# A transformer block in fp4 emulation on one core: negated scales made by GpSimd, ten zero products, the last tile normalised by VectorE, every queue re-sorted

## What is computed

```python
def reference(out, W_write, W_read, decay, log_alpha, w_gate, w_up, w_down):
    x = out                                     # (8, 512, 256) float32
    # chunked linear attention with a decay, read by r = x, written by w = x shifted by one
    v = x @ W_write.T
    reads = decayed_causal(x, shifted(x)) @ v   # scan over chunks in the reference
    attn = x + exp(log_alpha) * (reads @ W_read.T)
    x = layernorm(x + attn)
    # feed-forward, each operand rounded to fp4 blockwise (16 values share a scale)
    gate, y = fp4(x) @ fp4(w_gate).T, fp4(x) @ fp4(w_up).T     # 704 columns each
    h = silu(gate) * y
    return layernorm(x + fp4(h) @ fp4(w_down).T)
```

## Time and profile before

| | |
|---|---|
| median of 3 runs | 326.65 us (326.39 to 327.18) |
| the profiled execution, own time | 326.19 us |
| span of that execution in the profile | 324.5 us |
| instructions in the profile | 6515 |
| TensorE busy | 314.7 us, 97% |
| VectorE busy | 293.5 us, 90% |
| GpSimd busy | 239.9 us, 74% |
| ScalarE busy | 210.8 us, 65% |
| read from and written to HBM | 11.08 MB and 4.19 MB |

### The profile page before, as it was taken

One profiled execution on the slowest core, in us unless ns is written; L12 is line 12 of the kernel. 1 busy time (PEld: TensorE's weight loads), 2 busy tenths in 40 slices (PEclk: granted clock), 3 DMA queues, 4 the chain that ended last, 5 costly groups with the idle time before them and its releaser, 6 DMA issues.

```text
span 324.5 us, 6515 instructions
## 1 busy us (share of the span) xinstructions
PE 314.7 (97%) x2065; PEld 285.2 (88%) x2065; DVE 293.5 (90%) x754; ACT 210.8 (65%) x516; POOL 239.9 (74%) x257
## 2 busy tenths in 40 slices
PE   8999999999999999999999999999999999999993
PEld 3899888979988999899999999899989889999983
DVE  4999898999898999698996989999999999999982
ACT  7378977594915786348926687466657745665774
POOL 1869859857975789956996688687677767569672
PEclk9999999999999999999999999999999999999999
DMA  6821300210010202020010200020000000001002
GB/s 230 295 67 67 128 3 0 68 66 2 1 65 18 82 2 75 24 81 20 32 68 16 83 1 33 2 81 17 18 2 33 18 0 33 19 16 34 33 31 69
DMA packets 8242, 15.69 MB, mean 48 GB/s; under 512 B 1040, under 2 KB 5136, under 8 KB 8208
## 3 DMA queue, kind: packets, MB, share of 16 engines
q1 hardware_dynamic: 7920, 15.01, 13.5%
q10 hardware_dynamic: 288, 0.26, 0.3%
HBM read 11.08 MB, written 4.19 MB: 47 GB/s over the span
## 4 chain that ended last, share of the span: by engine, by line
PE 70%; DVE 18%; issue 6%; ACT 4%; POOL 1%; DVEq 0%; POOLq 0%; ACTq 0%
PE gu L1690 11%; PE gu L1694 11%; PE gu L1691 11%; PE bank L1690 5%; PE bank L1691 5%; PE bank L1694 5%; PE bank L1778 4%; DVE h_y L1071 3%; PE bank L1700 2%; PE bank L1703 2%; PE bank L1704 2%; DVE w_raw L1182 2%; PE bank L1752 2%; PE gu L1825 2%; DVE hqT_lo L1209 2%
## 5 line engine op out<-in xcount | busy, mean ns | idle before, releaser
L410 POOL TENSOR_TENSOR h_q<-h_g,h_ns 128x704 f32<-128x704 f32 x32 | 47.3, 1477 | 39.5 <-DVE h_g L1076 36.0
L1690 PE MATMUL gu<-guT_hi,xqT_hi 128*128 128x512 f32 (+1 forms) x192 | 74.9, 390 | 0.5 <-DVE w_raw L1182 0.5
L1691 PE MATMUL gu<-guT_lo,xqT_hi 128*128 128x512 f32 (+1 forms) x192 | 72.1, 376 | 0.0
L681 ACT ACTIVATE w_raw<-gu 128x512 f32<-128x512 f32 x64 | 29.3, 461 | 47.2 <-PE gu L1694 46.8
L1694 PE MATMUL gu<-guT_hi,xqT_lo 128*128 128x512 f32 (+1 forms) x192 | 56.7, 377 | 0.5 <-DVE xqT_lo L1173 0.5
L403 POOL TENSOR_TENSOR h_n<-w_raw,h_rs 128x704 f32<-128x704 f32 x32 | 49.0, 1531 | 9.3 <-DVE h_rs L1066 8.8
L1690 PEld LDWEIGHTS gu<-guT_hi,xqT_hi 128*128 128x128 f32 x192 | 36.1, 188 | 6.7 <-issue 1.3
L1694 PEld LDWEIGHTS gu<-guT_hi,xqT_lo 128*128 128x128 f32 x192 | 35.6, 188 | 6.7 <-DVE xqT_lo L1173 0.9
L1691 PEld LDWEIGHTS gu<-guT_lo,xqT_hi 128*128 128x128 f32 x192 | 36.2, 188 | 5.2
L1071 DVE SCALAR_TENSOR_TENSOR h_y<-h_sq,h_n 128x704 f32<-128x704 bf16 x34 | 36.3, 1069 | 1.6 <-ACT h_sq L685 1.5
L1182 DVE TENSOR_TENSOR w_raw<-w_raw,gu 128x512 f32<-128x512 f32 x64 | 32.3, 506 | 2.9 <-ACT w_raw L681 2.2
(11 more groups left out here) (156 smaller groups left out, 941.1 us busy)
## 6 DMA issues: line engine op xcount, KB each, us to landing
xs<-in_x_rows_dram SPq DMA_DIRECT2D x8, 512.0 KB, 3.3
out_dram<-wq_gu SPq DMA_DIRECT2D x32, 128.0 KB, 1.7
x_full<-in_xt_rows_dram SPq DMA_DIRECT2D x7, 512.0 KB, 3.3
w_raw<-in_w_ffn_dram SPq DMA_DIRECT2D x6, 352.0 KB, 5.9
w_pair<-in_w_attn_dram SPq DMA_DIRECT2D x1, 512.0 KB, 5.1
x_full<-in_xt_rows_dram SPq DMA_DIRECT2D x1, 256.0 KB, 2.8
x_full<-in_xt_rows_dram ACTq DMA_DIRECT2D x1, 256.0 KB, 3.4
scal<-in_scalars_dram ACTq DMA_DIRECT2D x1, 1.0 KB, 1.7
```

The lines of the kernel that those rows point to most:

```text
L410: nc.gpsimd.tensor_tensor(blocks(h_q[:, p, 0:I]), blocks(h_g[:, p, :]), per_block(h_ns[:, p, :], HB), ALU.mult).then_inc(h_quant, 1)
L681: nc.scalar.activation(silu[:, p, part[half]], gate_of[half], ACT.Silu).then_inc(silu_ready, 1)
L1690: nc.tensor.matmul(dst, lh, rh, start=(first and i == 0), stop=False)
L1691: nc.tensor.matmul(dst, lh, rl, start=False, stop=False)
```

## The change

1. `h_ns` is made by GpSimd in a new step `h_neg_scales`; `h_divisors` on VectorE makes `h_sc` alone. The wait for the dequantisation of two tiles before moves from `h_divisors` to `h_neg_scales`, `h_maxima` waits for the negation of two tiles before as well, and `h_dequant` waits for the negation of its own tile.
2. Ten products of zeros in place of 14.
3. The last tile (31) is normalised by VectorE in a new step `out_finish`, which adds the negated mean and multiplies by the power's result; GpSimd makes only the power for this tile, and the last store waits for `out_finish`.
4. The bank tables are changed (`combine` goes to `bank[0]`), and the lists on all engines, SP's loads included, are re-sorted. The steps themselves and their number stay, apart from the above.

```diff
-        s_bank, r_bank = (gu[:, 3, :], bank[0], bank[3], gu[:, 3, :]), (bank[2], bank[1])
-        h_bank = ((bank[1], bank[0]), (bank[1], bank[0]), (bank[2], gu[:, 3, :]), (bank[3], gu[:, 3, :]))
-        d_bank = (bank[3], bank[0], bank[2], gu[:, 3, :])
+        s_bank, r_bank = (bank[3], gu[:, 3, :], bank[0], gu[:, 3, :]), (bank[0], bank[3])
+        h_bank = ((bank[3], gu[:, 3, :]), (bank[1], bank[2]), (bank[0], gu[:, 3, :]), (bank[0], bank[2]))
+        d_bank = (bank[3], bank[2], bank[1], bank[0])
...
-            store(31, 3)
+            sp.wait_ge(o_last, 1)
+            sp.dma_start(out_rows[31], o_out[:, 3, :]).then_inc(stored[3], 16)
...
+            def h_neg_scales(k, p):
+
+                pool.wait_ge(h_amax, k + 1)
+                if k >= 2:
+                    pool.wait_ge(h_quant, k - 1)
+                nc.gpsimd.tensor_scalar(h_ns[:, p, :].rearrange("p (r c) -> p r c", c=4), h_am[:, p, :, 0:4], -1.0 / FP4_MAX,
+                                        -SCALE_FLOOR, ALU.mult, ALU.min).then_inc(h_negated, 1)
+
             def h_dequant(k, p):
                 pool.wait_ge(h_grid, k + 1)
+                pool.wait_ge(h_negated, k + 1)
...
-            out_rstd(31, 1)
+            pool.wait_ge(o_var, 32)
+            nc.gpsimd.tensor_tensor(o_rstd[:, 1:2], o_ve[:, 1:2], neg_half[:, 0:1], ALU.pow).then_inc(o_rstd_ready, 1)
...
                 if k >= 2:
                     dve.wait_ge(h_div, k - 1)
+                    dve.wait_ge(h_negated, k - 1)
...
             def h_divisors(k, p):
-                if k >= 2:
-                    dve.wait_ge(h_quant, k - 1)
-                divisors(h_am[:, p, :, 0:4], h_sc[:, p, :], h_ns[:, p, :], h_amax, h_div, k + 1)
+                dve.wait_ge(h_amax, k + 1)
+                nc.vector.tensor_scalar(rows_like(h_sc[:, p, :], h_am[:, p, :, 0:4]), h_am[:, p, :, 0:4], NUDGE / FP4_MAX,
+                                        SCALE_FLOOR * NUDGE, ALU.mult, ALU.max).then_inc(h_div, 1)
...
+            def out_finish(k, b, t):
+
+                p = t % 2
+                c = slice(p, p + 1)
+                dve.wait_ge(o_var, k + 1)
+                dve.wait_ge(o_rstd_ready, k + 1)
+                dve.wait_ge(stored[t], b * 16 + 16)
+                nc.vector.tensor_scalar(o_out[:, t, :], o_z[:, p, :], o_nm[:, c], o_rstd[:, c], ALU.add,
+                                        ALU.mult).then_inc(o_last, 1)
...
-            for _ in range(14):
+            for _ in range(10):
                 nc.tensor.matmul(gu[:, 3, :], zeros[:, 0:P], zeros[:], start=True, stop=True)
...
             gate_up(31, 7, 3, 0)
+            h_transpose(27, 3, 1, [(o_ready, 26)])
+            down(26, 2, [(hT_lo_ready, 51)])
             gate_up(31, 7, 3, 1)
```

More of the change, by code:

```diff
@@ L1384, in _ @@
-            out_moments(0, 0)
-            h_rest(2, 2, 0)
-            x_divisors(2, 1)
-            h_rest(2, 2, 1)
+            hidden(4, 0, 0)
+            h_magic_add(2, 0)
+            x_to_grid(1, 1)
+            hidden(4, 0, 1)
+            out_residual(0, 0)
+            h_rest(1, 1, 0)
+            h_reciprocals(3, 1)
+            h_to_grid(2, 0)
+            h_maxima(4, 0)
+            hidden(5, 1, 0)
+            x_residual(3, 0)
+            x_divisors(2, 0)
+            h_divisors(4, 0)
@@ new lines, in _ @@
+            x_to_grid(6, 1)
+            hidden(23, 1, 0)
+            hidden(23, 1, 1)
+            x_residual(7, 1)
+            h_to_grid(21, 1)
+            h_magic_add(22, 0)
+            out_residual(18, 2)
+            h_rest(19, 3, 0)
+            h_maxima(23, 1)
+            h_rest(19, 3, 1)
+            h_divisors(23, 1)
+            x_reciprocals(7, 0)
+            h_reciprocals(23, 1)
+            h_rest(20, 0, 0)
+            out_residual(19, 3)
+            out_moments(18, 0)
+            x_moments(7, 1)
@@ L1836, in _ @@
             values(0, 1, [])
[L1837 to L1847 removed]
+            reads(0, 0, [(pr_ready, 3)])
```

1379 lines of the change are left out of this document (690 added, 689 removed).

## The result

The changed kernel takes 331.07 us (median of 4 runs, 330.87 to 331.52) against 326.86 (326.39 to 327.18): a ratio of 1.0144, interval 1.0130 to 1.0159. It is 4.2 us slower by the medians and 4.7 by the ratio. The prediction was 325.4 with a range up to 327.6. Two executions in later groups took far longer than all others (384.71 us, the kernel before, and 794.93 us, e17) and are left out of every ratio.

What follows compares the result with a forecast made beforehand. TensorE was taken as the bound (97% busy), VectorE a close second. Terms -0.56 - 0.80 + 0.60 - 0.50 = -1.26 us took the profiled 326.19 us to 324.93, as a median 325.4 us, range 323.6 to 327.6.

Steps and rivals of the forecast that it cites:

- Banks and orders, -0.80 us: Re-sorted queues and banks, 10 to 300 us: fewer TensorE gaps ended by VectorE, 0.8 us off, between 0 and 2.8.
- new gaps of the same size: Rival: every gap removed has a new one, so the orders give nothing; 326.7 us, or 326.2 with start kept; chance 0.25.
- the idle 2.8 us: TensorE's idle time from 10 to 300 us, taken as all that any order of work could win there.
- VectorE's busy time lower by up to 6 us: Sign expected in the profile after, from 32 `h_ns` instructions of 190 ns leaving VectorE.
- Start, -0.56: Kernel start: with ten zero products the first score product starts at about 5.87 us, scores end 0.56 us earlier; bounds 0 to 0.95.
- It doesn't wait: Start: the product needing `w_pair` finds its load landed at 7.1 us, so TensorE does not wait.
- Negation, 0: Negated scales on GpSimd: about 0 directly, 32 instructions at 0.3 us each, 10 us, hidden in GpSimd's free time.
- Last two tiles, +0.60: End: tile 30's dequantisation wait goes (-0.30 us), a stall before tile 31's transposes comes (+0.90, range 0.2 to 1.5).
- last tile, -0.50: Chain after tile 31's power: VectorE's single normalisation takes 0.40 us instead of 0.90; saving between 0.23 and 0.62.
- the gate behind `down(26)`: Tile 31's narrow gate product, now after `down(26)`, leaves TensorE 8.0 us of work before tile 31's transposes instead of 10.1.
- wait for `out_residual` in each pass: Slow rival: `reads(n, 1)` waits for the residual in loop passes, three to five waits of 0.8 us; 327.8 to 329.4; chance 0.13.
- the clock rose: Slow rival: TensorE's pause at 5.5 us moves the clock's rise behind the `w_pair` product, +2.3 us, 327.7 us; chance 0.07.

Runs made afterwards that it cites:

- e17: Kernel before with x's moments made column by column and h's negated scales made on GpSimd: 326.27 us, ratio 0.9998.
- e1: Changed kernel with the negated scales back on VectorE, new orders and banks kept: ratio 1.0139 to the kernel before.
- e3: Kernel before with only ten zero products and the last tile normalised by VectorE: ratio 0.9977 to the kernel before.
- e11: Kernel before with ten zero products, last tile normalised by VectorE, and x's moments made column by column: 321.78 us, ratio 0.9865.
- e13: Changed kernel with x's moments made column by column and the negated scales back on VectorE: 326.95 us, ratio 1.0017.
- e12: Kernel before with x's moments alone changed, four VectorE instructions of 128x1 in place of two of 128x2: 321.78 us, ratio 0.9869.
- e8: Changed kernel with x's moments made column by column, four instructions of 128x1 in place of two of 128x2: 327.57 us, ratio 1.0046.
- e2: Kernel before with the negated scales on GpSimd alone, order and banks otherwise untouched: ratio 1.0052.
- e6: Changed kernel with the narrow gate product of tile 31 ahead of `down(26)` again: 331.30 us, ratio 1.0157.
- e15: e8 with tile 31's gate and up ahead of `down(26)` and its VectorE steps moved ahead: 328.51 us, ratio 1.0072.
- e5: Changed kernel with `v_rest(1, 0)` ahead of x's moments and divisors on VectorE: 330.41 us, ratio 1.0128.
- e9: Changed kernel with the two remainders of the second sequence's x ahead of `w_to_grid(0)` on VectorE: 331.46 us, ratio 1.0162.
- e10: e8 with the three order moves of e5, e6 and e9 together: 328.20 us, ratio 1.0070.
- e14: e8 with the first 20 us of VectorE's and GpSimd's lists back in the old order: 328.13 us, ratio 1.0061.
- e16: e8 with the edits of e14 and e15 together: 328.82 us, ratio 1.0082.
- e18: e13 with the rest of x^T, then weight tile 0's grid and the scores, ahead of weight tile 1's grid on VectorE: 330.05 us, ratio 1.0128.

## Why the prediction was wrong

**The step that failed is "Banks and orders, -0.80 us".** It measured +5.3 us, by e1 against e3. The prediction itself listed tight places in both orders and said that it couldn't price each; it then took the sign from VectorE's lighter load. Its rival "new gaps of the same size" had the right mechanism, new gaps where VectorE is late, but kept them to the size of the old ones. The bound was the fault: the idle 2.8 us was taken for the size of what an order can change, and nothing bounds what it can lose. By the windows the middle lost 7.52 - 2.80 = 4.7 us. Even for a gain the 2.8 us aren't a bound. Between e3 and e11 TensorE's idle time over the span fell by 2.7 us (10.4 to 7.7) and its busy time by 2.0 (314.1 to 312.1), with the same products: some waits seem to lie hidden in what counts as busy. The prediction had said that its rows are a lower bound, and didn't use it.

**"VectorE's busy time lower by up to 6 us" was wrong**, and the lighter load was the reason given for the sign. It rose by 8.2. The prediction named the shared interfaces and saw 1.39 and 2.10 us for one instruction in the earlier trace rows, then let it alter nothing because 128x44 elements are few. The length of the small instruction isn't the price. What counts is what its partner does: a VectorE instruction of 0.1 us lasted up to 1.36, and a new order decides anew which instructions meet. How much of the loss these meetings make isn't shown. Their sum doesn't set it: it was 9.0 us between e3 and e1 and 4.7 between e11 and e13, for nearly the same loss. A single meeting at a bad place can count, like the two `xT_lo` of the changed kernel:

```profile
16.03 2.48 DVE L1142 TENSOR_TENSOR xT_lo<-x_full,xT_hi 128x512 fp32r<-128x512 f32 x2
...
16.10 1.87 POOL L362 TENSOR_TENSOR wq_gu<-h_g,h_ns 128x704 f32<-128x704 f32 x1
```

The two took 1.29 us in the kernel before, and TensorE waits for the second.

**Start, -0.56.** The number came near, the ten zeros didn't make all of it. The `w_pair` products start at 7.71 instead of 8.39, 0.68 us earlier. But e12, with all 14 zero products, has them at 7.70, and e1, with ten, at 8.14. The term took the clock's rise as fixed at about 7.0 us; it moves from execution to execution (last section). Where it came as late as in the kernel before, in e8, ten zeros gave 8.39 - 7.93 = 0.46 us, near the term; where it came early they gave nothing. "It doesn't wait" for `w_pair` failed in e3, where TensorE waited 0.20 us for that load and went on at 8.08. Over many executions the start and the last tile together gave 0.75 us (e3), and nothing measurable with the columns (e11 against e12). The lower bound, 0, was a fair one.

**Negation, 0.** Right by the result (e1 to after), wrong by its working: 545 ns each, not 300, 17.4 us and not 10. In the old order it costs 1.7 us (e2) and, with the columns, some 3.7 to 4.2 (e17).

**Last two tiles, +0.60; last tile, -0.50.** The wait in front of tile 31's transposes came (0.91 in the trace, forecast 0.2 to 1.5):

```profile
320.06 1.04 PE L1826 MATMUL bank<-ident,h_q 128*128 128x128 f32 x6 [0.91 <-DVE hqT_lo L1248]
...
326.54 0.55 POOL L621 TENSOR_TENSOR o_rstd<-o_ve,neg_half 128x1 f32<-128x1 f32 x1 [0.86 <-DVE o_ve L1264]
327.19 0.41 DVE L1274 TENSOR_SCALAR wq_gu<-wq_gu,o_nm,o_rstd 128x256 f32<-128x256 f32 x1 [0.72 <-DVE o_ve L1264]
```

From the power's end (327.09) to the last element (327.60) are 0.51 us, not 0.40, so 0.39 saved and not 0.50. TensorE's idle time after 300 us grew by 6.03 - 5.77 = 0.26; with the 0.39 added back the two tiles cost 0.65, against 0.60. That agreement is luck in part: there is also a wait of 0.38 us in front of `down(28)`, which the prediction didn't have. And e6 and e15 show that the named reason, the gate behind `down(26)`, isn't what sets the wait: with the gate ahead it is still 0.96 us in e6 and 0.78 in e15. In e3 the start and the last tile together gave 0.75 us of the forecast 1.06.

**The rivals.** No wait for `out_residual` in each pass (two in all, 0.7 and 0.3 us), and the clock rose before the `w_pair` products, not behind them: neither slow rival happened. The slower case that did happen had no line of its own.

**Open.** Which decisions of the new order cost the 5 us, and whether the banks or the lists do. The whole list of TensorE, VectorE, GpSimd or ScalarE can't be put back by itself: by the counts of the semaphores, with the other lists new, the engines wait for one another in a circle. SP's list, the order of the loads, can be, and no run tried it; no wait of the changed kernel's TensorE is for a DMA, which speaks against it as the cause. The moves within the new order (e5, e6, e9, e10, e14, e15, e16, e18) gained nothing that stands clear of their intervals; where the trace was read, a wait taken away at one place returned at another. The best kernels of the study are e11 and e12, 321.78 us: the old order with the moments made column by column, 1.3% under the kernel before.

## What to carry to other kernels

A re-sorting of an order that leaves its bounding engine 1% idle has little to gain and no bound on what it can lose; don't take its sign from a lighter load on one engine, and don't take the idle share for a strict bound on the gain either (e11 gained 3.7 us on e3, where 3.1 were idle in the middle). Compare busy times over the same work and not over the same microseconds. Before an explanation is kept, make its edit in the other kernel as well: the columns gave back 3.2 us in the changed kernel and looked like the cause, and gave 3.7 us in the old one, where there was no loss to explain. Read a group's mean against its quickest member: an instruction over two elements with a mean of 414 ns, with its neighbour `z_ve`, was worth 3.7 us and was there to be seen in the kernel before.
